# The gate of the tiles' feed-forward stage in one Trainium2 kernel, with tanh in the place of silu

## What is computed

```python
x = x + _L0_xattn_ref(_layernorm(x), ctx_1024, ...)
x = x + _L0_attn_ref(_layernorm(x), W_attn, W_proj)
x = x + _L0_ffn_ref(_layernorm(x), ...)
# inside _L0_ffn_ref, for every row:
x1 = jnp.einsum('btd,hd->bth', x, sw1) + sb1
x2 = jnp.einsum('btd,hd->bth', x, sw2) + sb2
sh = _ln(jax.nn.silu(x1) * x2, s_ln_g, s_ln_b)
shared_out = jnp.einsum('bth,dh->btd', sh, sw3) + sb3
```

## Time and profile before

| what | us |
|---|---|
| median of 3 runs (lowest, highest) | 1576.93 (1576.16, 1578.63) |
| the profiled execution's own time | 1577.39 |
| its span, first to last instruction | 1575.6 |
| PE busy | 1435.8 (91%) |
| DVE busy | 1071.0 (68%) |
| ACT busy | 571.4 (36%) |
| POOL busy | 438.7 (28%) |

### The profile page before, as it was taken

One profiled execution on the slowest core, in us unless ns is written; L12 is line 12 of the kernel. 1 busy time (PEld: TensorE's weight loads), 2 busy tenths in 40 slices (PEclk: granted clock), 3 DMA queues, 4 the chain that ended last, 5 costly groups with the idle time before them and its releaser, 6 DMA issues.

```text
span 1575.6 us, 31857 instructions
## 1 busy us (share of the span) xinstructions
PE 1435.8 (91%) x13465; PEld 896.6 (57%) x13465; DVE 1071.0 (68%) x2154; ACT 571.4 (36%) x999; POOL 438.7 (28%) x466
## 2 busy tenths in 40 slices
PE   7078999999999999999999999999999999998678
PEld 3046566655666666566665666666566665664333
DVE  4716777777777777777777777777777777775535
ACT  1412434333433434433433333433443433343221
POOL 0012323333223333323332322323333333322111
PEclk9589999999999999999999999999999999999769
DMA  9143322332333333332332333333332332335410
GB/s 366 60 187 136 124 98 109 135 111 105 129 135 135 135 135 135 129 107 106 123 120 100 124 135 135 135 135 135 132 116 98 120 130 101 114 135 225 144 61 20
DMA packets 36349, 201.32 MB, mean 128 GB/s; under 512 B 4968, under 2 KB 5864, under 8 KB 25712
## 3 DMA queue, kind: packets, MB, share of 16 engines
q1 hardware_dynamic: 36208, 199.29, 34.4%
HBM read 182.24 MB, written 17.04 MB: 126 GB/s over the span
## 4 chain that ended last, share of the span: by engine, by line
PE 45%; DVE 25%; issue 8%; POOL 8%; ACT 7%; DMA 0%; DVEq 0%; SPq 0%; POOLq 0%
POOL rstd L635 8%; PE ps_a L1132 8%; DVE stats L818 7%; PE ps_t L1124 4%; PE ps_a L1166 4%; PE ps_a L1223 4%; PE ps_v L1143 4%; PE ps_t L1143 3%; DVE rows L831 3%; ACT L753 2%; DVE rows L824 2%; PE ps_a L1188 2%; PE ps_t L1254 2%; PE ps_a L1178 2%; DVE mv L819 2%
## 5 line engine op out<-in xcount | busy, mean ns | idle before, releaser
L644 POOL TENSOR_TENSOR act_l<-act_t,act_h 128x512 f16<-128x512 f32 x192 | 217.0, 1130 | 397.1 <-ACT act_t L687 397.1
L635 POOL TENSOR_TENSOR rstd<-var,mhalf 128x1 f32<-128x1 f32 x224 | 170.5, 761 | 563.9 <-DVE var L820 563.9
L679 ACT ACTIVATE act_h<-ps_t,scale 128x512 f16<-128x512 f32 (+1 forms) x160 | 103.6, 647 | 201.7 <-PE ps_t L1124 201.6
L1124 PE MATMUL ps_t<-ident,rows 128*128 128x128 f32 x512 | 83.1, 286 | 45.0 <-DVE rows L824 42.2
L1132 PE MATMUL ps_a<-wproj,act_t 128*128 128x512 f32 x256 | 120.1, 613 | 0.7 <-ACT act_t L749 0.7
L1132 PE MATMUL ps_a<-wcv,act_t 128*128 128x512 f32 x256 | 115.3, 593 | 0.2 <-ACT act_t L693 0.2
L818 DVE BATCH_NORM_STATS2 stats<-rows 128x6 f32<-128x512 f32 x160 | 111.1, 695 | 5.5
L702 ACT ACTIVATE p_n<-rows,ntop 128x128 f32<-128x128 f32 x32 | 12.9, 402 | 269.3 <-DVE ntop L855 269.3
L687 ACT ACTIVATE act_t<-ps_t,scale 128x512 f32<-128x512 f32 (+1 forms) x160 | 103.0, 644 | 0.0
L1143 PE MATMUL ps_a<-w_parts,act_h 128*128 128x512 f16 x384 | 95.9, 387 | 2.1 <-ACT act_h L679 2.1
L1124 PEld LDWEIGHTS ps_t<-ident,rows 128*128 128x128 f32 x512 | 56.3, 143 | 69.3 <-DVE rows L824 66.2
(11 more groups left out here) (246 smaller groups left out, 2908.3 us busy)
## 6 DMA issues: line engine op xcount, KB each, us to landing
ctx_t<-in_ctx_t SPq DMA_DIRECT2D x32, 2056.0 KB, 8.4
ctx_n<-in_ctx_n SPq DMA_DIRECT2D x32, 2048.0 KB
x_in<-in_x SPq DMA_DIRECT2D x32, 256.0 KB, 9.4
ctx_last<-in_ctx_last SPq DMA_DIRECT2D x32, 256.0 KB
x_scratch<-rows SPq DMA_DIRECT2D x32, 256.0 KB, 8.9
out<-rows SPq DMA_DIRECT2D x32, 256.0 KB, 2.2
wattn_f<-in_wattn SPq DMA_DIRECT2D x1, 3072.0 KB, 19.8
wattn<-in_ew SPq DMA_DIRECT2D x6, 512.0 KB, 8.6
```

What stands on the lines that cost most here:

```text
L635: nc.gpsimd.tensor_tensor(rstd[s][:], var[s][:], mhalf[:], ALU.pow).then_inc(rstd_ready[s], 1)
L644: nc.gpsimd.tensor_tensor(act_l[s][:, chunks], act_t[s][:, chunks], act_h[s][:, chunks], ALU.subtract).then_inc(act_l_ready[s], 1)
L679: nc.scalar.activation(act_h[s][:, 0:width // P].rearrange("p c r -> p (c r)"), bank[s][:, 0:width], ACT.Copy, scale=scale[:, k:k + 1]).th ...
L1124: mm = nc.tensor.transpose(out[s][:, c * P:(c + 1) * P], rows[s][:, lo + c * P:lo + (c + 1) * P], ident[:])
```

## The change

`silu(u) v` is written as `(tanh(u/2) + 1) (u v / 2)`. ACT computes the tanh with an input scale of 0.5, in the place of the Silu. DVE computes h = 0.5 u v right behind `rows2` (a new instruction with both tensor inputs in SBUF, written to `v_n`, columns 256:512), and later z = (tanh + 1) h with one instruction in the place of the product. The new instruction waits for `u_ready`, and what follows it on DVE waits for its own chain step.

```diff
-         "out_norm": 3, "head_scores": 2, "head_total": 1, "head_weights": 1, "project_out": 2, "silu": 4, "ffn_out": 1}
+         "out_norm": 3, "head_scores": 2, "head_total": 1, "head_weights": 1, "project_out": 2, "ffn_in": 1, "silu": 4, "ffn_out": 1}
...
                 def ffn_in(s, r, tile):
                     act.wait_ge(u_ready[s], r + 1)
-                    nc.scalar.activation(v_n[s][:, 0:H], rows2[s][:, 0:H], ACT.Silu).then_inc(gate_ready[s], 1)
+                    nc.scalar.activation(v_n[s][:, 0:H], rows2[s][:, 0:H], ACT.Tanh, scale=0.5).then_inc(gate_ready[s], 1)
...
                     nc.vector.scalar_tensor_tensor(rows2[s][:], ps_a[s][:], unscale[:, K_W12:K_W12 + 1], b12[:],
                                                    ALU.mult, ALU.add).then_inc(u_ready[s], 1)
+                    dve.wait_ge(u_ready[s], r + 1)
+                    chain = Chain("ffn_in", s, r)
+                    chain(nc.vector.scalar_tensor_tensor(v_n[s][:, H:], rows2[s][:, 0:H], 0.5, rows2[s][:, H:],
+                                                         ALU.mult, ALU.mult))
+                    chain.end()
...
                     z = v_n[s][:, H:]
-                    chain(nc.vector.tensor_tensor(z, v_n[s][:, 0:H], rows2[s][:, H:], ALU.mult))
+                    chain(nc.vector.scalar_tensor_tensor(z, v_n[s][:, 0:H], 1.0, z, ALU.add, ALU.mult))
```

## The result

| | before | after |
|---|---|---|
| median, us | 1576.93 | 1584.88 (1582.74 to 1586.24, 5 runs) |
| the profiled execution's own time | 1577.39 | 1583.80 |
| its span | 1575.6 | 1582.0 |
| mean granted TensorE clock | 0.966 | 0.972 |

The changed kernel is slower: ratio 1.005, 95% interval 1.0035 to 1.0064. Run again beside the experiments it had a median of 1584.16, ratio 1.0058 (1.0035 to 1.0081).

A forecast was written before the change was run, and what follows sets the result against it. PE bounds the steady round, through `turn_z` waiting for z. 30 steady rounds x 0.30 us = +9.0 us on the profiled 1577.39 gives 1586.4; the median, 0.46 below, is 1585.9 us (+0.57%), range 1582.5 to 1593.

The forecast's parts named there:

- What sets the round: z's product on DVE sets `turn_z` on PE, and that the steady round; PE waits 0.55 us for z.
- rival B: Slack before the product, or between `turn_z` and the next norms, pays the hold: about 1576.9 us; 6%.
- Table loads worth nothing here: Without the load the tanh ends at 781.40, not 782.33, but the held chain starts the product at 782.67.
- Durations: Half product and new product on DVE take 0.426 us each; the tanh on ACT takes the Silu's 0.417.
- Hold: Half product on DVE starts 0.23 us inside POOL's remainder (L644), is held and ends at 782.13, not 781.41.
- A: Half product is not held, POOL gives way; z 0.42 us earlier, 12.6 us gained, 1564.3 us; 8%.
- C: Hold lasts until the remainder's recorded end; +0.50 us a round, +15.0 us, 1591.9 us; 6%.
- Rival D: A table load stays before the tanh, or tanh is slow; 1585.9 us as well, no chance of its own.
- Size of the hold: Half product is held until 781.70, 0.20 us before the remainder's recorded end; low bound took 0.26 us.
- What stands behind it: On DVE behind the half product: maximum 0.41 us, L878 0.15, product at 782.67; z 0.30 us later.
- The rest of the time: Outside the 30 steady rounds: 0 for tile 30's round and 0 for the last tile.

The follow-up runs named there:

- one SBUF tensor: Changed kernel, with the half product reading u from the PSUM bank `ps_a` instead of `rows2`: 1560.82 us, ratio 0.9899 to the kernel before.
- behind the maximum: Changed kernel, with the half product moved behind the maximum of the context scores on DVE: 1570.86 us, ratio 0.9960 to the kernel before.
- PSUM: Kernel before, with tanh gate, u and v written back to PSUM, z made in two DVE steps, no half product: 1559.91 us, ratio 0.9901.
- late remainder: Changed kernel, with GpSimd's remainder of the other tile (L644) waiting for the new product: 1573.82 us, ratio 0.9986 to the kernel before.
- half product alone: Kernel before, with Silu, table loads and old product kept and only the half product added: 1585.26 us, ratio 1.0054.
- tanh alone: Kernel before, with tanh(u/2) in place of the Silu and the old product kept: 1560.32 us, ratio 0.9896.

## Why the prediction was right, point by point

- **What sets the round.** Right, and rival B (the delay is absorbed on the way) fell with it. In six kernels the round followed `turn_z` to 0.01 us: +0.38 and +0.38 (changed kernel), -0.39 and -0.39 (one SBUF tensor), -0.14 and -0.14 (behind the maximum), -0.50 and -0.49 (PSUM), -0.04 and -0.04 (late remainder), +0.37 and +0.37 (half product alone). Where PE stops waiting, it gets 0.59 us a round, not 0.55.
- **Table loads worth nothing here.** Right, shown by the half product alone. That they are worth 0.59 us a round where the product can follow was not in the prediction; it spoke only of the limit.
- **Durations.** The half product's bare 0.424 us and the tanh's 0.416 were right (0.426 and 0.417 forecast).
- **Hold.** Right in kind, and the rivals A (POOL gives way) and C (hold until the recorded end) fell. A's mechanism is real all the same: it is decided by who starts first, and in one round of 30 DVE did. Rival D (a load is left or the tanh is slow) fell with L753: no load, and 0.416 us.
- **Size of the hold.** The term that was too small. I took the release at 0.20 us before the recorded end of the remainder, from L827 and L831, which have pointer scalars (`mv`, `rstd`). For such instructions 0.20 us holds: the scaling of z, held in the rounds of the late remainder, is released 0.20 us before that end as well. The half product has immediates alone, and this form is released 0.14 us before it, in every steady round of the traces in which it or the old product is held (here 786.64 - 786.51 = 0.13 by the rounded times). Why the two forms differ was not tested. So the half product ends at 1.98 us, not 1.92; that it starts at 0.79 us and not 0.77 costs nothing, since it is held either way.
- **What stands behind it.** The maximum takes 0.43 us when it has waited for its predecessor, not 0.41 as when it started ahead of its end. With the gaps the product starts at 2.55, not 2.46. In all 0.38 us a round and not 0.30: 30 rounds make 11.4 us, not 9.0.
- **The rest of the time.** I put nothing there, and it was not nothing. Between the profiles lie 6.4 us: +11.1 in the 29 steady distances, -0.6 before them, -0.8 in the two rounds behind them, and -3.3 from the last L987 to the end (72.2 to 68.8). Without the last part the profiled execution would have taken 1587.1 us.
- **Luck.** The median, 1584.88 us, lies 1.0 us below the forecast of 1585.9, closer than its terms deserve. By the profiles the steady rounds cost 2.1 us more than the 9.0 forecast, and 4.7 us that had no term came back outside them; the two errors partly cancel.

That last part has a place in the trace. These are two windows of 10 us each from the last L987 on, before (columns: stretch, length, then busy time and count of PE, PEld, DVE, ACT, POOL, then the granted clock, DMA share, GB/s):

```profile
1503.40:1513.40 10.00, 4.70 (x15) 2.37 (x15) 6.13 (x13) 2.39 (x5) 1.94 (x3) 0.64 0.08 27
1513.40:1523.40 10.00, 10.00 (x22) 5.04 (x23) 2.84 (x13) 1.24 (x4) 0.00 (x0) 0.68 0.15 52
```

and with the change:

```profile
1513.15:1523.15 10.00, 4.60 (x15) 2.24 (x16) 6.56 (x14) 2.29 (x5) 1.94 (x3) 0.66 0.08 26
1523.15:1533.15 10.00, 8.90 (x26) 3.88 (x25) 2.93 (x14) 3.29 (x7) 0.00 (x0) 1.00 0.16 53
```

In the second window the granted clock was 1.00, which is 2.4 GHz, with the change, and 0.68 before, a mean of that level and of 1.2 GHz. In both kernels PE was busy for less than half of the window ahead of it. The first product of the experts there (eight matmuls on `wqk`) took 6.23 us before and 3.68 after. Of the nine profiles, seven have 68.7 to 69.1 us from the last L987 to the end; those of the kernel before and of the tanh alone have 72.2. These two are also the ones in which the last tile's product starts 1.23 us behind the last L987; in the other seven it starts at 1.30 us or later. Of the 15 runs of the kernel before that stood beside the last three experiments, four took 1572.1 to 1572.6 us and eleven 1576.6 to 1579.2, so one program can have both. What chooses was not tested. Both profiles of the changed kernel fell on the short side, and its nine runs lie between 1582.74 and 1586.24 us without two such groups; whether it falls there more often than the kernel before, by its own timing, stays open.

## What to carry to other kernels

Ahead of putting work on an engine that has idle time, look at what its neighbour does in that window: here a VectorE instruction with two tensors in SBUF did not go on while GpSimd had a subtraction of two SBUF tensors that began first, so 0.42 us of work took 1.19, and the round grew by 0.38. Leave one of the two tensors in PSUM, or put such an instruction behind others that read PSUM, and the hold is gone or filled. One SBUF tensor is no pass by itself: L1032, a `tensor_scalar` from SBUF to SBUF, was held too. And the removal of a table load is worth what then ends earlier, not the length of the load: here nothing with the half product in front, and 0.59 of 2.57 us a round alone.

## What the runs showed of the hardware that I had not expected

- The hold ends at one moment, whenever the held instruction came: three starts between 0.79 and 1.24 us, all released at 1.56 or 1.57 us, 0.14 us before the recorded end of GpSimd's instruction. With pointer scalars it is 0.20 us.
- Which engine waits is decided within less than 0.1 us: VectorE ahead by 0.06 us ran free and GpSimd took 1.39 us; VectorE behind by 0.25 us was held for 0.77 us, and L1032, behind by 0.02 us, for 0.39. The Trainium skill (SBUF — State Buffer, "Who interferes with whom") says that issue order decides, and this round agrees.
- An instruction of VectorE that writes its result back into the PSUM bank it reads costs nearly the same as one that writes to SBUF: L987 took 0.76 us there and 0.75 before.
